# A decoder layer on one core: every step, chunk and group written out straight in place of hardware loops

## The reference

```python
a  = rope_attention(x, wq, wk, wv)                    # 16 heads of 16, no mask
x1 = layernorm(x + a)
c  = attention(x1 @ Wq.T + bq, ctx @ Wk.T + bk, ctx @ Wv.T + bv, mask) @ Wo.T + bo
x2 = layernorm(x1 + c)
gates = softmax(x2 @ router_w + router_b)             # 8 experts, the best 2 of each token
h   = gelu(buf @ w1 + b1)                             # buf: at most 1280 tokens of an expert
out = layernorm(x2 + sum over chosen e of gates[e] * (h @ w2 + b2)[e, position])
```

## Time and profile before

| | |
|---|---|
| median of 3 runs | 2501.18 us (2500.62 to 2502.72) |
| the profiled execution, its own time | 2499.03 us |
| its span, first to last instruction | 2497.3 us |
| mean granted clock of TensorE | 0.924 of full speed |
| instructions executed | 52990 |
| PE busy | 2220.8 us (89%), 18752 matmuls |
| DVE, ACT, POOL busy | 1249.2, 974.0 and 586.3 us |
| attention, experts, combine | 0 to 1786 us, 1786 to 2418, 2418 to 2497 |

### The profile page before, as it was taken

The page is one execution under the profiler, slowest core; times in us unless marked ns, Lnnn a source line. Parts: engine busy times, 40 slices in busy tenths (PEclk is TensorE's granted clock), DMA queues, the critical chain, the costliest instruction groups (busy, mean ns, idle before and its releaser), DMA issues. The chain is left out here.

```text
span 2497.3 us, 52990 instructions
## 1 busy us (share of the span) xinstructions
PE 2220.8 (89%) x18752; PEld 1533.9 (61%) x18752; DVE 1249.2 (50%) x2596; ACT 974.0 (39%) x1474; POOL 586.3 (23%) x910
## 2 busy tenths in 40 slices
PE   5899999999999999999999999988399999999940
PEld 3566666666666666666666666655277777777730
DVE  3366666666666666666666666653111111111116
ACT  0254555455554555445545555542122122122100
POOL 0012222322223222232223222221112122122122
PEclk7799999999999999999999999987599999999975
DMA  8001100010001000000000000000223233133126
GB/s 247 9 15 31 35 30 26 30 40 26 22 23 33 30 26 20 23 29 24 19 21 24 29 23 19 24 21 11 67 66 76 71 79 67 26 73 78 15 55 231
DMA packets 111837, 113.43 MB, mean 45 GB/s; under 512 B 12096, under 2 KB 107405, under 8 KB 111776
## 3 DMA queue, kind: packets, MB, share of 16 engines
q1 hardware_dynamic: 85792, 85.87, 11.2%
q0 software_dynamic: 17664, 18.35, 4.3%
q10 hardware_dynamic: 8320, 8.39, 1.0%
HBM read 64.53 MB, written 56.05 MB: 48 GB/s over the span
## 5 line engine op out<-in xcount | busy, mean ns | idle before, releaser
L835 DVE TENSOR_REDUCE smax<-ps_s 128x4 f32<-128x1024 f32 x512 | 625.7, 1222 | 458.1 <-PE ps_s L555 430.6
L718 ACT ACTIVATE prob<-ps_e 128x1024 f32<-128x1024 f32 x512 | 524.0, 1024 | 654.1 <-PE ps_e L564 593.1
L555 PE MATMUL ps_s<-stack 17*128 17x256 f32 x4096 | 593.1, 407 | 74.8 <-ACT stack L706 45.8
L564 PE MATMUL ps_e<-stack 18*128 18x256 f32 x4096 | 594.9, 409 | 11.9 <-ACT prob L718 11.6
L555 PEld LDWEIGHTS ps_s<-stack 17*128 17x128 f32 x4096 | 359.8, 188 | 287.4 <-issue 185.7
L564 PEld LDWEIGHTS ps_e<-stack 18*128 18x128 f32 x4096 | 358.2, 188 | 27.8 <-ACT prob L718 15.6
L580 PE MATMUL ps_w<-prob,val 128*32 128x256 f32 x4096 | 302.6, 446 | 25.4 <-DVE val L847 25.4
L1403 ACT ACTIVATE hid<-m_ps_h,b_sb 128x320 f32<-128x320 f32 x256 | 134.9, 527 | 431.5 <-PE m_ps_h L1365 431.5
L1365 PE MATMUL m_ps_h<-m_cols,w_sb 128*128 128x320 f32 x1024 | 280.3, 435 | 0.6 <-DVE m_cols L1415 0.6
L1379 PE MATMUL m_ps_o<-w_sb,hid 128*128 128x256 f32 x1280 | 279.1, 379 | 0.6 <-ACT hid L1403 0.6
L1379 PEld LDWEIGHTS m_ps_o<-w_sb,hid 128*128 128x128 f32 x1280 | 242.2, 190 | 33.1 <-ACT hid L1403 1.1
(11 more groups left out here) (120 smaller groups left out, 2178.7 us busy)
## 6 DMA issues: line engine op xcount, KB each, us to landing
w_sb<-in_w SPq DMA_DIRECT2D x16, 1024.0 KB, 7.6
slot_rows_dram<-fill SPq DMA_DIRECT2D x8, 1290.0 KB, 14.5
m_rows<-slot_rows_dram SPq DMA_DIRECT2D x16, 645.0 KB, 7.2
xT<-in_xT SPq DMA_DIRECT2D x32, 256.0 KB, 2.6
ctxT<-in_ctxT SPq DMA_DIRECT2D x32, 256.0 KB, 2.6
x_res<-in_x SPq DMA_DIRECT2D x32, 256.0 KB, 2.7
stack<-nrows SPq DMA_DIRECT2D x512, 2.0 KB
sums_dram<-x SPq DMA_DIRECT2D x32, 256.0 KB, 2.2
```

Source lines behind the costliest of these rows:

```text
L555: mm = nc.tensor.matmul(ps_s[:, s_bank(X, p), t, :], stack[X][rows, Q, p // HG, t * P:(t + 1) * P], stack[X][rows, K, p // HG, :], start=T ...
L564: mm = nc.tensor.matmul(ps_e[:, p % 2, t, :], stack[Y][rows, K, h // HG, t * P:(t + 1) * P], stack[Y][rows, Q, h // HG, :], start=True, st ...
L718: nc.scalar.activation(prob[:, h:h + 2, :].rearrange("p h s -> p (h s)"), ps_e[:, :, :, :].rearrange("p h t s -> p (h t s)"), ACT.Exp, sca ...
L835: nc.vector.tensor_reduce(max_columns(X, p), ps_s[:, :, :, :], AX.X, ALU.max)\
```

## The change

`slots_of` runs `step(i)` for all 35 steps in a Python loop, `turns` runs its four chunks four times, and `in_pairs` emits all groups one by one, so every engine's stream is written out in full. The order of the work, the tiles, the transfers and the semaphores stay as they are; all counts and addresses become constants. With no loop variable left, PE's bank bookkeeping needs no reset, and `readers_after` goes.

```diff
-        loop_first = 4
...
-            last_full = NB - 2
-            for i in range(loop_first):
-                step(i)
-            with eng.Fori(loop_first, last_full + 1) as i:
-                step(i)
-            for i in range(last_full + 1, NB + 3):
+            for i in range(NB + 3):
                 step(i)
...
-        def readers_after(i):
-
-            return {bank(name, T, k): reader(name, T, i + o, k) for name, T, k, o in uses}
...
             def emit(i, X, Y, bX, bY):
-                if X == SELF and (not isinstance(i, int) or loop_first <= i < NB):
-                    held.update(readers_after(i - 1))
                 a = at[X]
...
 def in_pairs(eng, n, emit):
 
-    emit(0, 0)
-    emit(1, 1)
-    with eng.Fori(1, n // 2 - 1) as i:
-        emit(i * 2, 0)
-        emit(i * 2 + 1, 1)
-    emit(n - 2, 0)
-    emit(n - 1, 1)
+    for q in range(n):
+        emit(q, q % 2)
...
-            four(0)
-            with eng.Fori(1, CHUNKS // 4 - 1) as i:
+            for i in range(CHUNKS // 4):
                 four(i)
-            four(CHUNKS // 4 - 1)
```

## The result

The changed kernel takes 2477.35 us (median of 4 runs, 2468.47 to 2478.68) against 2501.28 for the kernel before beside it (4 runs, 2500.62 to 2502.72): a ratio of 0.9896, 95% interval 0.9873 to 0.9919. The profiled execution took 2468.47 us, the shortest of the four. Lines have moved: score matmuls L555 and L564 are now L545 and L554, the values matmuls L580 are L570, DVE's copy L847 is L835, ScalarE's (ACT) exponential L718 is L706.

A forecast was written before the change was run, and what follows sets the result against it. TensorE (PE), busy 89% of the 2497.3 us span, was taken as the bound up to the end of the experts. Attention 2.0 + experts 0.8 + last stage 0.4 = 3.2 us, median 2501.18 to 2498.0; range 2486 to 2505.

The forecast's parts named there:

- Branch: Attention loop: removing PE's branch, 0.21 us taken 27 times, is worth 0, since the wait for DVE's copy grows instead.
- The cover: Before L580: PE's wait for DVE's copy of the values hides the branch; without it the branch is worth 16.7 us.
- Rival C: Attention: the cover of L847 goes and 0.62 us a step come through, 17.9 us in all, 2483.3; chance 0.03.
- Waits: Attention loop: constants replace wait values computed in registers, 0.22 us of a step, between 0 and 5.9 us.
- The period: Attention: low clock stretches 51.2 us apart limit the waits' gain to a slide of some 2.0 us, not 5.9.
- The pricing of a low stretch: At L580, once a step, the clock falls to 1.2 GHz; its 32 matmuls take 3.56 against 1.94 us, costing 1.62.
- the loop's rest at 51.20: Attention loop: L580 has settled into a period of exactly 51.20 us, as far apart as the low clock stretches.
- Rival B: Attention: two to four steps escape the low clock, 1.62 us each, and 5.9 us come too: 11.9 us, 2489.3; chance 0.29.
- Instruction fetch: Attention: straight code fetches throughout, 100 more packets on q8, 55 on q14; cost 0 to 13.5 us, taken as 0.
- Rival D: DVE and ScalarE stall at newly fetched code, 0.25 us each, where PE waits: 6.4 us slower, 2507.6; chance 0.12.
- Experts and last stage: DVE's idle before the column copy falls to 16.63 us, POOL's before the inverse deviation to 6.34: 0.8 and 0.4 us saved.
- The stretch between attention and experts: After the attention loop, at a mean clock of 0.64: may come out 2 us either way.

The follow-up runs named there:

- two_steps: Kernel before with two attention steps in each pass of its loop, one branch in two steps: 2539.73 us, ratio 1.0146 to the kernel before.
- gap3_again: Changed kernel with three transposes right ahead of the first cross score matmul of every step: 2492.19 us, ratio 0.9963 to the kernel before.

## Why the prediction was wrong

**Branch: right.** Worth 0, as said: the cross half step is 26.60 us in the straight kernel and 26.61 in the loop. Before the first scores of the self half step PE is idle 0.31 us (0.31 was forecast), before L570 1.37 (1.38):

```profile
538.82 0.48 PE L545 MATMUL ps_s<-stack 17*128 17x256 f32 x2 [0.31 <-ACT stack L694]
```

The cover, DVE's copy, holds in every step. Rival C didn't happen.

**Waits: right in size.** A self half step with a low stretch is 24.34 us (24.37 forecast) against 24.59. The 0.20 us between a low-free step in `two_steps` and a straight one is the same term without a branch, so most of the 0.25 is not the branch; that it is the computed waits is the one difference left that I know of, and no run changes them alone.

**The period: this step failed.** The prediction had the slide end "when the low stretch has moved past L580 (its 1.94 us) and the idle time comes to lie so that the clock stays down longer in one step, which sets it back", and collected 2.0 us. The opposite came: the stretch slides from 0.27 us ahead of L570's first matmul to 0.83 behind it, 1.1 us and not 1.94, then drops out, and what sets it back are three short steps. So 17 of the 24 us are low-free steps, and the waits' 0.26 us, which the prediction set aside as mere slide, are gained in every other step too. The pricing of a low stretch (1.62 forecast, 50.94 - 49.31 = 1.63 measured) and the loop's rest at 51.20 were right. The error was to forecast a turn for which no row existed, and to put it on the side on which nothing changes. Steps 0 to 3 of the trace of before gave the slide, not its end; the honest bounds of the term were 0 and all that low-free steps give, and my range took in only two to four of them.

**Rival B had the outcome, and its count was mis-sized.** "Some steps of about 49.4 us without a low stretch" is what the trace shows, 49.31. B counted that each pass of the slide frees one step, from 0.22 us a step; it frees three, and the passes are shorter, so 9 of 27 came instead of 2 to 4. With 9, B's own terms make 27 x 0.25 + 9 x 1.63 + 1.2 = 22.6 us, and 23.9 were measured. The remark against it, that 1.7 us of idle time within 3 is hard to split, was no evidence: the idle time was the same in both kinds of step, and that it is split where the clock stays up is not shown either.

**Instruction fetch: right.** 105 packets on q8 and 50 on q14 between 317 and 1580 us (100 and 55 forecast), and no cost on PE but, if it is one, the 0.6 us in step 13. Rival D's stall of 0.25 us a step isn't there. What I hadn't asked is what a loop with a larger body would cost.

**Experts and last stage: right.** 16.63 and 6.34 us in the chunks and groups that were in the loops, as in the others; from the first expert matmul to the end 1.4 us less, 1.2 forecast. The stretch between attention and experts, which I allowed 2 us, gave about 2.5 and up to 9: it hangs on how long the clock is at its lower level there, 122.4 us before, 102.1 in the shortest execution and 111.4 to 115.5 in the other three.

## What to carry to other kernels

Where a loop's step keeps pace with a steady spacing of low clock stretches, as here, a change of a fraction of a microsecond is worth either nothing or whole stretches: print step lengths over the whole run, price a low stretch, and let the range reach to the case in which they drop out; in `gap3_again` even longer steps were faster in sum. A pad tests a period only where nothing can absorb it. Before unrolling a hardware loop in part, look for instruction packets at its turns: here a body of one step had none and no stall, a body of two stalled at each turn, and the fully straight form had packets but no such stall.

## What was not expected of the hardware

- A loop body of two attention steps waits 4.66 us on the mean at every turn, with instruction packets around it (12 of 12), a body of one step never does (0 packets in 1278 us), and straight code fetches 4.2 packets a step without a wait.
- A straight step 0.48 us longer than the changed kernel's still ran 9 us faster than the loop, with 10 of 27 steps at a granted clock of 1.00.
- Three transposes ahead of the score matmuls cost 0.48 us a step; one or three of them elsewhere cost nothing.
- On two of the chips ACT's exponential behind L570 starts 0.8 us late in nearly every step from step 3 or 4 on, and low-free steps are 1.2 us longer than on another chip for the same program (50.96 against 49.79). Its cause is open.
